# Four transformer blocks on one core: where the row sums of the 64-wide heads are taken, and a new order of work in the 16-wide attention

## The reference, cut to what matters

```python
def attention_L0(x):                       # 16 heads of 64; L3: the same with normed q and k
    q, k, v = split(x @ W_qkv)
    attn = einsum('bqhd,bkhd->bhqk', q, k) * 64 ** -0.5
    attn = softmax(attn, axis=-1)          # exp(s - row maximum) / row sum
    out = einsum('bhqk,bkhd->bqhd', attn, v)
    return out @ W_out + b_out

def attention_L2(x, node_mask):            # 16 heads of 16
    scores = einsum('bhnd,bhmd->bhnm', q, k) * 16 ** -0.5
    scores = where(mask, scores, -inf)
    out = einsum('bhnm,bhmd->bhnd', softmax(scores), v)
    return out @ proj_w + proj_b
```

## Time and profile before

| | before |
|---|---|
| runs, us | 3335.65, 3476.47, 3338.05 |
| median, us | 3338.05 |
| profiled execution, us | 3335.07 |
| its span, us | 3333.3 |
| mean granted TensorE clock | 0.96 |
| TensorE busy | 3028.1 us, 91% |
| VectorE busy | 2154.0 us, 65% |
| ScalarE busy | 1694.8 us, 51% |
| GpSimd busy | 915.1 us, 27% |

### The profile page before, as it was taken

The page is one execution under the profiler, slowest core; times in us unless marked ns, Lnnn a source line. Parts: engine busy times, 40 slices in busy tenths (PEclk is TensorE's granted clock), DMA queues, the critical chain, the costliest instruction groups (busy, mean ns, idle before and its releaser), DMA issues. The chain is left out here.

```text
span 3333.3 us, 70757 instructions
## 1 busy us (share of the span) xinstructions
PE 3028.1 (91%) x26089; PEld 2516.2 (75%) x26090; DVE 2154.0 (65%) x4193; ACT 1694.8 (51%) x3085; POOL 915.1 (27%) x725
## 2 busy tenths in 40 slices
PE   7999999997998989999999699799999999994697
PEld 5887888775998979877777598577777777772586
DVE  4655565655666766567777566757575757567775
ACT  3444444443554445554455345566666666662364
POOL 2232323232112231122222211322222222221574
PEclk8999999998999999999999799899999999997799
DMA  5000000001001000000000100100000000004243
GB/s 171 4 6 6 6 3 6 6 6 36 19 19 46 0 23 0 22 4 9 9 9 9 46 19 19 36 1 0 0 0 0 0 0 0 0 1 130 80 126 86
DMA packets 68976, 80.66 MB, mean 24 GB/s; under 512 B 10146, under 2 KB 61090, under 8 KB 68884
## 3 DMA queue, kind: packets, MB, share of 16 engines
q1 hardware_dynamic: 62756, 71.14, 7.4%
q0 software_dynamic: 6144, 8.52, 1.4%
HBM read 66.80 MB, written 12.85 MB: 24 GB/s over the span
## 5 line engine op out<-in xcount | busy, mean ns | idle before, releaser
L956 POOL TENSOR_TENSOR L3a_shift<-L3a_neg,L3a_mx 128x256 fp32r<-128x256 f32 x128 | 94.7, 740 | 523.1 <-DVE L3a_mx L1556 523.1
L1063 ACT ACTIVATE L0a_prob<-L0a_st 128x512 f32<-128x512 f32 x256 | 134.0, 602 | 160.4 <-PE L0a_st L1293 72.6
L945 POOL TENSOR_TENSOR L0a_o<-L0a_prob 128x1024 f32<-128x1024 f32 x48 | 118.8, 2475 | 302.6 <-PE L0a_o L1330 302.6
L1063 ACT ACTIVATE L3a_prob<-L3a_st 128x512 f32<-128x512 f32 x256 | 133.8, 602 | 117.8 <-POOL L3a_o L945 90.0
L1925 ACT ACTIVATE L2a_prob<-L2a_st 128x512 f32<-128x512 f32 x256 | 132.2, 604 | 117.7 <-PE L2a_st L1958 117.7
L1556 DVE TENSOR_REDUCE L0a_mx<-L0a_s 128x2 f32<-128x512 f32 x224 | 143.8, 683 | 73.9 <-PE L0a_s L1267 73.9
L1546 DVE SCALAR_TENSOR_TENSOR L3a_qk_lo<-raw,cols_sb,L3a_qk_hi 128x256 fp32r<-128x256 f32 x256 | 157.9, 656 | 36.5 <-ACT L3a_qk_hi L1054 36.5
L1556 DVE TENSOR_REDUCE L3a_mx<-L3a_s 128x2 f32<-128x512 f32 x256 | 163.7, 679 | 15.5 <-PE L3a_s L1267 15.5
L2190 DVE TENSOR_REDUCE L2a_mx<-L2a_s 128x2 fp32r<-128x512 f32 x256 | 163.5, 681 | 15.2 <-PE L2a_s L1958 15.2
L1157 PE MATMUL L0a_st<-L0a_xt,home 128*128 128x256 f32 x512 | 150.1, 293 | 5.1 <-DVE home L1664 5.1
L1158 PE MATMUL L0a_st<-L0a_xt,home 128*128 128x256 f32 x512 | 145.6, 284 | 0.0
(11 more groups left out here) (615 smaller groups left out, 11241.6 us busy)
## 6 DMA issues: line engine op xcount, KB each, us to landing
raw<-in_moe_w SPq DMA_DIRECT2D x16, 1024.0 KB, 8.6
x_sb<-in_x SPq DMA_DIRECT2D x1, 4096.0 KB, 24.9
L0a_gate<-gate_rows SPq DMA_DIRECT2D x32, 128.0 KB, 3.9
L0m_gate<-gate_rows SPq DMA_DIRECT2D x32, 128.0 KB, 3.8
L2a_gates<-gate_rows SPq DMA_DIRECT2D x32, 128.0 KB, 3.9
L2m_gate<-gate_rows SPq DMA_DIRECT2D x32, 128.0 KB, 3.8
out_x<-x_sb SPq DMA_DIRECT2D x1, 4096.0 KB, 17.0
token_rows<-x_sb SPq DMA_DIRECT2D x1, 4096.0 KB, 29.3
```

The lines of the kernel that those rows point to most:

```text
L945: nc.gpsimd.tensor_tensor(half_sums, both[:, :, :, 0:N], both[:, :, :, N:2 * N], ALU.add).then_inc(halves_done, 1)
L956: nc.gpsimd.tensor_tensor(shift[:, u % 4, :, :, :], neg64[:].unsqueeze(1).unsqueeze(1).to_broadcast([P, 2, TT, 64]), mx[:, u % 2, :, :].un ...
L1063: A(prob[:, u % 4, h, :], st_ps[u % 2][h][:], ACT.Exp, scale=64 ** -0.5).then_inc(p_done, 1)
```

## The change

In heads64 the halves on GpSimd and their semaphore are gone, ScalarE's two waits for them too, and all four sets of sums are taken from all exponentials: 8 multiplications each, `sums(p - 1)` right behind `column_part(p - 1)`, the last, `sums(3)`, ahead of `column_part(3)`. In heads16 the transposed scores of a slot are interleaved over both pairs of heads (except in slot 1, where the second pair still waits for x_low), so slot 3 waits for `taken` ahead of both; `over` comes behind the projection and the maxima rows on TensorE and behind shift and qk_low on VectorE; x_low moves from the end of slot 0 to between the two maxima at the start of slot 1; o_low(0) and both o_high move by a few places.

```diff
@@ -938,12 +937,6 @@
                     gated_wait(wo_hi, n + 1)
                     nc.gpsimd.tensor_tensor(wo[1][:, cs, :], src, wo[0][:, cs, :].bitcast(F32), ALU.subtract).then_inc(wo_done, 1)
-            def halves(i, p):
-
-                gated_wait(pv_done, PAIRS * i + p + 1)
-                both = prob[:, 2 * p % 4:2 * p % 4 + 2, :, :]
-                nc.gpsimd.tensor_tensor(half_sums, both[:, :, :, 0:N], both[:, :, :, N:2 * N], ALU.add).then_inc(halves_done, 1)
-
             if qknorm:
                 nc.gpsimd.memset(var_sel[:], 0.0).then_inc(sel_made, 1)
                 gated_wait(sel_made, 1)
...
@@ -959,11 +952,8 @@
                 def body(i):
                     for u in range(6):
                         shift_of(i, u)
-                    halves(i, 0)
                     shift_of(i, 6)
                     shift_of(i, 7)
-                    halves(i, 1)
-                    halves(i, 2)
                 token_rstd(1)
                 output_weights()
...
@@ -1098,8 +1086,6 @@
                 for p in range(PAIRS + 1):
                     if p == 1 and not final:
                         act.wait_ge(xlo_done, i + 2)
-                    if p in (2, 3):
-                        act.wait_ge(halves_done, 3 * i + p - 1)
                     if p < PAIRS:
                         exp(2 * p, 0)
                         exp(2 * p, 1)
...
@@ -1332,20 +1318,17 @@
                                           skip_group_check=True)
                     last.then_inc(pv_done, 1)
-                def sums(p, halved):
-
-                    if halved:
-                        pe.wait_ge(halves_done, 3 * i + p + 1)
-                    else:
-                        pe.wait_ge(p_done, 2 * (U * i + 2 * p) + 4)
-                    for kt in range(1 if halved else TT):
+                def sums(p):
+
+                    pe.wait_ge(p_done, 2 * (U * i + 2 * p) + 4)
+                    for kt in range(TT):
                         for odd in range(2):
                             for h in range(2):
                                 at = 64 * odd + 32 * h
                                 last = mm(sum_ps[at:at + 32, 0:N], sum_sel[:, p, :],
-                                          half_sums[:, odd, h, :] if halved else prob[:, (2 * p + odd) % 4, h, kt * N:(kt + 1) * N],
-                                          start=(p == 0), stop=(p == 2), skip_group_check=True)
-                    if p == 2:
+                                          prob[:, (2 * p + odd) % 4, h, kt * N:(kt + 1) * N],
+                                          start=(p == 0 and kt == 0), stop=(p == 3), skip_group_check=True)
+                    if p == 3:
                         last.then_inc(sums_done, 1)
                 def last_over(n):
...
@@ -1422,16 +1405,14 @@
                 values(3)
                 for p in range(1, PAIRS):
                     row_part(p)
-                    if p >= 2:
-                        sums(p - 2, True)
                     column_part(p - 1)
+                    sums(p - 1)
                 if not final:
                     pe.wait_ge(xlo_done, i + 2)
                     pe.wait_ge(p_done, 2 * (U * i + 6) + 1)
                     qk(0, i + 1)
-                sums(3, False)
+                sums(3)
                 column_part(3)
-                sums(2, True)
             transposes(0)
             pe.wait_ge(pre, 2)
...
@@ -1928,13 +1909,12 @@
                         A(v[:, :, :, 0:16], v_ps[:].rearrange("p (t h d) -> p t h d", t=TT, d=16), ACT.Copy).then_inc(v_done, 1)
                         if not first:
                             row_high(i - 1)
-                    if u == 1 and not first:
-                        o_high(i - 1, 0)
                     if u == 0 or not final:
                         qk_high(U * i + u + 3, (u + 3) % U, 0)
                     if u == 0 and not final:
                         x_hi(i + 1)
                     if u == 1 and not first:
+                        o_high(i - 1, 0)
                         o_high(i - 1, 1)
                     if u % 2:
                         act.wait_ge(pv_done, PIECES * i + u // 2 + 1)
...
@@ -2026,15 +2006,16 @@
                 last.then_inc(mxt_done, 1)
             def body(i, first, final):
-                def scores_t(w):
+                def scores_t(u, pairs):
                     for kt in range(TT):
                         ks = slice(N + kt * P, N + (kt + 1) * P)
                         for n, (a, b) in enumerate(((qk_hi, qk_hi), (qk_lo, qk_hi), (qk_hi, qk_lo))):
-                            for h in range(2):
-                                last = mm(st_ps[w % 2][h][:, kt * N:(kt + 1) * N], a[rows(w, h), w // 2, ks], b[rows(w, h), w // 2, 0:N],
-                                          start=(kt == 0 and n == 0), stop=(n == 2))
-                                if kt == TT - 1 and n == 2:
-                                    last.then_inc(st_done, 1)
+                            for w in pairs:
+                                for h in range(2):
+                                    last = mm(st_ps[w][h][:, kt * N:(kt + 1) * N], a[rows(w, h), u, ks], b[rows(w, h), u, 0:N],
+                                              start=(kt == 0 and n == 0), stop=(n == 2))
+                                    if kt == TT - 1 and n == 2:
+                                        last.then_inc(st_done, 1)
                 def values():
                     for tt in range(TT):
...
@@ -2061,12 +2042,14 @@
                         pe.wait_ge(v_done, i + 1)
                     if u == 2 and not first:
                         pe.wait_ge(on_done, PIECES * i)
-                    scores_t(2 * u)
                     if u == 1 and not final:
+                        scores_t(u, (0,))
                         pe.wait_ge(xlo_done, i + 2)
-                    if u == 3 and not first:
-                        pe.wait_ge(taken, i)
-                    scores_t(2 * u + 1)
+                        scores_t(u, (1,))
+                    else:
+                        if u == 3 and not first:
+                            pe.wait_ge(taken, i)
+                        scores_t(u, (0, 1))
                     if u == 0 and not first:
                         gather_sums(i - 1)
                     if ahead:
...
@@ -2075,10 +2058,6 @@
                     if u == 0:
                         pe.wait_ge(p_done, 4 * slot + 2)
                         values()
-                    if u == 1 and not first:
-                        pe.wait_ge(p_done, 4 * slot + 3)
-                        over(i - 1, 0)
-                        over(i - 1, 1)
                     if u == 0 or not final:
                         pe.wait_ge(p_done, 4 * slot + 1)
                         if u == 1:
...
@@ -2089,6 +2068,10 @@
                         if u == 1 and not first:
                             pe.wait_ge(rsum_done, i)
                         max_rows(u + 1)
+                    if u == 1 and not first:
+                        pe.wait_ge(p_done, 4 * slot + 3)
+                        over(i - 1, 0)
+                        over(i - 1, 1)
                     if beyond:
                         pe.wait_ge(qkhi_done, slot + 3)
                         scores(2 * slot + 4, 2 * u + 4)
...
@@ -2182,9 +2165,9 @@
                 dve.wait_ge(qkhi_done, chunk + 1)
                 V.tensor_tensor(qk_lo[:, c, :], ring[bank][:], qk_hi[:, c, :].bitcast(F32), ALU.subtract).then_inc(qklo_done, 1)
-            def maxes(pair, w):
-
-                for h in range(2):
+            def maxes(pair, w, heads=(0, 1)):
+
+                for h in heads:
                     dve.wait_ge(s_done, 2 * pair + h + 1)
                     at = 64 * (w % 2) + 32 * h
                     V.tensor_reduce(mx[:, w // 2 % 2, :, at], s_ps[h][:].rearrange("p (t n) -> p t n", t=TT), AX.X, ALU.max).then_inc(mx_done, 1)
...
@@ -2199,29 +2182,31 @@
                 for u in range(U):
                     slot = U * i + u
                     ahead = not final or u < U - 1
-                    if ahead:
+                    if ahead and u == 1 and not final:
+                        maxes(2 * slot + 2, 2 * u + 2, (0,))
+                        x_low(i + 1)
+                        maxes(2 * slot + 2, 2 * u + 2, (1,))
+                    elif ahead:
                         maxes(2 * slot + 2, 2 * u + 2)
                     if u == 0 and not first:
                         reciprocals(i - 1)
                     if u == 2 and not first:
-                        o_low(i - 1, 1)
+                        o_low(i - 1, 0)
                     if u == 3 and not first:
                         moments(i - 1)
                     if ahead:
                         maxes(2 * slot + 3, 2 * u + 3)
                     if u == 0 and not first:
                         row_low(i - 1)
+                    if u == 2 and not first:
+                        o_low(i - 1, 1)
+                    if ahead:
```

(11 more changed lines are left out.)

5 lines of the change are left out of this document (1 added, 4 removed).

## The result

The changed kernel takes 3294.59 us (median of 4 runs, 3292.74 to 3297.09) against 3336.85 us before. The ratio is 0.9875, with a 95% interval from 0.9856 to 0.9895: 1.25% faster. One of the four runs before, 3476.47 us, lies far above the others, and the ratio leaves it out. Forecast were 3310 us and a range of 3293 to 3333; the direction is right and the time lies in the range, near its low end. The gain is 42 us (41 without that run), where I had summed up 28.6.

What follows compares the result with a forecast made beforehand. TensorE, busy 92% in L2a and L3a, was taken as the bound. L0a +6.9, L3a -15.5, tails -2.5 and L2a -17.5 summed to -28.6 us, giving 3310 us, range 3293 to 3333.

Steps and rivals of the forecast that it cites:

- Added multiplications: L0a and L3a row sums on TensorE: four whole sets of 1.00 us instead of 2.71 us, +1.29 us per sequence.
- (a): TensorE's waits for GpSimd's halves, two per sequence, go away: 0.86 us per sequence in L0a, 1.18 in L3a.
- (e): L3a: without GpSimd's halves VectorE's low parts are no longer delayed; 0.15 us per sequence gained.
- (b): L3a: sums cover the wait for VectorE's maxima behind the first value product, 0.44 us per sequence; nothing in L0a.
- (c): L3a: last sums ahead of the last value product end the wait before the reciprocals' spreading, 0.49 us per sequence.
- (d): ScalarE's exponentials no longer wait for the halves; TensorE never waited for these, so nothing is gained.
- Tails: Last sequence of each stage: sums complete sooner before the output, -1.0 us in L0a and -1.5 in L3a.
- The rival that VectorE is freed: Third rival, chance 0.12: each half removed in L3a frees 1.0 us of VectorE, up to 32 us more, 3278 us.
- the walk through slot 1: L2a: reordering shortens slot 1 from 7.41 to 6.3 us, a gain of 1.1 per sequence.
- My 17.5 us: L2a's whole gain: 1.2 us in each of 14 middle sequences and about 1 us for first and last.
- Four tiles at once: L2a interleaved scores: by the skill's rule 1.19 us could halve in three slots, 29 us; prediction expected next to none.
- a new wait for the first exponential ahead of each projection: Sign expected in L2a's later profile if right: TensorE waits there for ScalarE after the faster interleaved scores.

Runs made afterwards that it cites:

- e3: The changed kernel with three GpSimd additions per sequence put back, reading unchanging weights, nothing waiting until VectorE's next output product: 3301.16 us.
- e7: The changed kernel with GpSimd halving the first two pairs again, each halved set behind the next value product, L0a's last sequence whole: 3286.15 us.
- e4: The changed kernel with the last pair's sums behind its value product instead of ahead of it: 3307.95 us.
- e5: The kernel before with only the transposed scores of L2a interleaved over four heads: 3330.68 us, one run.
- e6: The changed kernel with `over` back in its old places, ahead of maxima rows and shift, in L2a's last sequence only: 3293.59 us.
- e1: The kernel before with the heads64 part of the change alone: 3312.06 us.

## Why the prediction was right, and what it missed

**Added multiplications.** Right: 1.00 us a set in its new place, four sets, +1.29 us per sequence.

**(a) Waits for halves.** Right, in kind and in size. In L0a two sets lost 0.43 and 0.39 us, together 0.82 against my 0.86. In L3a the steps from the last rows of a score part to what follows give the price:

```profile
2496.48 0.28 PE L1293 MATMUL L3a_st<-L3a_shift,ones_r 64*128 64x256 f32 x2
...
2499.62 0.39 PE L1287 MATMUL L3a_st<-L3a_qk_hi 64*128 64x256 f32 x2
...
2502.79 0.42 PE L1345 MATMUL L3a_sum<-L3a_o,L3a_sum_sel 128*32 128x256 f32 x4 [0.60 <-POOL L3a_o L945]
```

The first set came 0.69 us behind that row (2496.48 to 2497.17) where the step is 0.21 now, the second 1.35 us behind the start of the last rows (2501.44) where it is 0.65 now (2474.51 to 2475.16). That is 0.48 and 0.70, together my 1.18.

**(e) VectorE's delay in L3a** is the term that was mis-sized. The two score parts of the earlier trace rows, up to the sums, took 3.38 and 3.17 us before, and take 2.58 and 2.29 now (2467.41 to 2469.99, 2472.87 to 2475.16). That is 1.68 us less per sequence, where I had 1.18 + 0.15: inside the parts 0.50 was lost and not 0.15. Only 0.18 of it lies in the second part, behind the blocked low parts. The other 0.32 lies in the first part, where TensorE met VectorE's results just as they were done, and no addition had blocked them:

```profile
2493.66 1.23 DVE L1546 SCALAR_TENSOR_TENSOR L3a_qk_lo<-raw,cols_sb,L3a_qk_hi 128x256 fp32r<-128x256 f32 x2
```

These low parts end at 2494.89 and the rows that need them start at 2495.03; the maxima behind them end at 2496.09 and the scores start at 2496.14. Now the low parts end 0.57 us ahead of their rows (2468.02 and 2468.59) and the maxima 0.31 ahead of the scores, since the microsecond of sums stands ahead of the part, as in (b). The prediction had given (b) the wait in front of the part and nothing inside it. e3 puts a price of only 0.10 on the additions once whole sums stand between; in e7, where they don't, the second part takes 2.98 us against 2.29, of which 0.43 is the wait for the low part. The cost of such a blocked engine depends on the slack that stands behind it.

**(b) and (c)** held: 0.52 us for the maxima (2.39 between product and scores, then 1.87) against 0.44, and 0.55 to 0.58 for the reciprocals (e4) against 0.49. I gave L0a nothing for (c); e4 says 0.16. With it L0a's sequence comes to +0.27, as measured (47.24 to 47.51), and not to +0.43.

**(d)** The exponentials without their wait: nothing in the rows speaks against it.

**Tails.** L3a about as forecast (1.9 us in e4, 1.5 taken). L0a was wrong in its cause and its size: not 1.0 us for an earlier reciprocal but about 5.8 for two places where GpSimd's additions held up VectorE's pieces of weights, with the slower clock behind the first (e3). The rival that VectorE is freed had this mechanism, but I looked for it in L3a's sequences only; it paid most at a place that occurs once. L0a and L3a beat my sum by 15 us: about 5 by this, 6 (0.35 per sequence) by (e) in L3a, the rest by (b) and (c). That the total still came into the range is in part luck: the 3 us that L2a in this profile is short of my sum offset a part of the 15, and without them the time would be about 3292, below the range. The third rival's price of 32 us in L3a's sequences didn't come.

**L2a.** Each step of the walk through slot 1 held. My 17.5 us was 2.9 too high for this profile, but close to what the four other kernels with this L2a show (17.0 to 17.2 us less than before). There was luck in that: I carried the gain of a middle sequence to the last, which loses some 3 us; the middle ones gave 1.25 for my 1.2, and the kernel before had a slow sequence of 1.5 us that I didn't count (last section). Four tiles at once, which the Trainium skill allows (TensorEngine Tiling (Array Packing), Theoretical Speedup), would by the prediction's estimate have made 29 us of the interleaving. e5 shows the 24 multiplications in 0.85 instead of 1.19 us, 1.4 times as fast and not twice, and 2 us of gain.

**The sign "a new wait for the first exponential ahead of each projection"** was half right. The waits of TensorE's weight loads in the middle of L2a (1440 to 1820 us) after the change:

```profile
PEld L2a_st L1938 <- ACT L2a_prob L1906: 13.4, 55, 0.4
PEld L2a_s L1938 <- DVE L2a_mx L2173: 9.2, 28, 0.3
```

In the kernel before these were 39 and 13 waits. So some sixteen new ones are for exponentials, about one per sequence and not one ahead of each projection, and fifteen for maxima ahead of the scores. In e5, with the interleaving alone, the totals of the two rise from 13.6 to 18.5 and from 5.5 to 15.7 us: this is where the faster scores went.

## What to carry to other kernels

A wait is two things: the time that it costs and the delays of other engines that it hides. Before moving work to end a wait, look up what the other engines finish just inside it; in L0a nothing was hidden, and the cheap form in a later place was best. In L3a a blocked VectorE was hidden, and results that came just in time, and the dearer form without GpSimd was best. Look at the last iteration by itself, since its cover is gone and other work (weights for the next stage) shares its engines.

## What the runs showed of the hardware

The clock of TensorE turned one lost wait into more. In the last sequence of L2a TensorE was idle for 1.58 and then 1.37 us in slot 1 of the changed kernel, where the kernel before has 1.23 and 0.23. The granted clock of that slot is 0.67 of full speed, where it was 1.00 before and 0.86 in e6: part of the slot ran at 1.2 instead of 2.4 GHz. From the start of the eight `over` multiplications to the next group it is 1.95 us there; in the other two kernels it is 1.45, and 0.23 and 0.24 of that are a wait for maxima. It can also come in the middle of a stage. In the kernel before one sequence of L2a lasted 30.31 us instead of 28.77, with this row for its first half:

```profile
1650.65:1664.11 13.46, 13.17 (x115) 11.63 (x115) 8.04 (x14) 5.44 (x10) 0.00 (x0) 0.87 0.00 0
```

Ahead of it TensorE had waited 0.46 us for an exponential, as in every sequence of that kernel. e1 has the same code in L2a and the same event in the same sequence, 30.29 us long:

```profile
1649.41:1662.87 13.46, 13.18 (x118) 11.65 (x119) 7.97 (x14) 5.45 (x10) 0.00 (x0) 0.87 0.00 0
```

None of the ten profiles with another order in L2a has a slow sequence in the middle. So 1.5 of the 14.6 us of L2a came from the clock. Whether the old order brings this about or two profiles fell alike isn't shown, and why the clock fell in this sequence stays open.

The other surprise is how exact the block between GpSimd and VectorE is: 3.42 us for a 1.22 us operation in two kernels, with different operands on GpSimd, and in e3 with no semaphore from the one to the other.
